# A 128-step state space convolution and a rewritten order of the joint round in a decoder kernel

## The reference, cut to what matters

```
x = layernorm(x_text);  x = x * (1 + gate * scale_in) + gate * shift_in
K = 2 * einsum('dn,dnl->dl', dC, powers).real            # one kernel of L = 256 steps for each channel
y = irfft(rfft(x, n=2L) * rfft(K, n=2L))[:, :L]          # a causal convolution over the 256 steps
y = y + x * D_skip
y = y * (1 + gate * scale_out) + gate * shift_out;  xt = x_text + y
h = gelu(layernorm(xt) @ W1 + b1) @ W2 + b2;  xt = xt + h
```

## Time and profile before

| what | value |
|---|---|
| median of 3 runs | 1935.76 us (1935.62 to 1937.24) |
| the profiled execution | 1936.92 us, span 1935.2 us |
| PE busy / PE weight loads busy | 1686.4 us (87%) / 1308.0 us (68%) |
| DVE / ACT / POOL busy | 1287.0 us (67%) / 864.3 us (45%) / 605.3 us (31%) |
| mean granted TensorE clock | 0.94 of 2.4 GHz |

### The profile page before, as it was taken

One profiled execution on the slowest core, in us unless ns is written; L12 is line 12 of the kernel. 1 busy time (PEld: TensorE's weight loads), 2 busy tenths in 40 slices (PEclk: granted clock), 3 DMA queues, 4 the chain that ended last, 5 costly groups with the idle time before them and its releaser, 6 DMA issues.

```text
span 1935.2 us, 26723 instructions
## 1 busy us (share of the span) xinstructions
PE 1686.4 (87%) x8210; PEld 1308.0 (68%) x8210; DVE 1287.0 (67%) x4141; ACT 864.3 (45%) x1675; POOL 605.3 (31%) x984
## 2 busy tenths in 40 slices
PE   5899999992299999982779999999999999999775
PEld 3677777771166677761658778778778778777654
DVE  3567777762148777334478888889888889876642
ACT  1444444440031111114556766667766667754321
POOL 1111111213300000005534445545444544433211
PEclk9899999995699999995789999999999999999987
DMA  9000000006644343425000000000000000000000
GB/s 272 3 1 1 1 1 1 1 1 234 249 137 137 110 119 99 134 77 197 12 6 1 12 12 6 12 6 12 12 12 6 12 6 7 6 6 1 6 6 11
DMA packets 81573, 94.11 MB, mean 49 GB/s; under 512 B 19142, under 2 KB 69527, under 8 KB 81179
## 3 DMA queue, kind: packets, MB, share of 16 engines
q1 hardware_dynamic: 72747, 78.91, 12.7%
q0 software_dynamic: 3072, 8.39, 1.2%
q10 hardware_dynamic: 5616, 5.11, 0.8%
HBM read 71.94 MB, written 20.45 MB: 48 GB/s over the span
## 4 chain that ended last, share of the span: by engine, by line
PE 35%; DVE 13%; ACT 2%; issue 2%; POOL 2%; POOLq 0%; ACTq 0%
PE E_pY L2313 6%; PE E_pK L2204 5%; PE E_pU L2303 4%; PE E_pK L2163 3%; PE E_pY L2151 3%; PE E_pS L2266 3%; PE E_pY L2284 3%; PE E_pU L2275 2%; DVE E_wk L1738 2%; DVE E_ex L1670 2%; DVE E_m L1731 1%; PE E_pY L2163 1%; PE E_pT L2145 1%; DVE E_num L1677 1%; PE E_pY L2214 1%
## 5 line engine op out<-in xcount | busy, mean ns | idle before, releaser
L1222 ACT ACTIVATE F_uT<-F_puT 128x1024 f32<-128x1024 f32 x39 | 39.9, 1024 | 294.3 <-PE F_puT L1282 294.3
L1492 POOL TENSOR_SCALAR E_var<-E_mv 128x2 f32<-128x2 f32 x80 | 34.2, 427 | 355.9 <-DVE E_mv L1607 355.7
L1273 PE MATMUL F_pu<-C_W,F_hT 128*128 x312 | 143.9, 605 | 0.3 <-issue 0.3
L1291 PE MATMUL F_py<-C_W,F_uT 128*128 x624 | 141.2, 379 | 1.2 <-ACT F_uT L1222 1.2
L1291 PEld LDWEIGHTS F_py<-C_W,F_uT 128*128 128x128 f32 x624 | 115.6, 190 | 16.0 <-issue 1.9
L2214 PE MATMUL E_pY<-E_Wcv,E_hid 128*128 128x256 f32 x512 | 118.7, 386 | 3.3 <-issue 3.3
L2303 PE MATMUL E_pU<-E_xT,E_W 128*128 128x256 f32 x512 | 117.7, 385 | 2.3 <-ACT E_xT L2052 2.3
L2313 PE MATMUL E_pY<-E_W,E_hid 128*128 128x256 f32 x512 | 118.1, 379 | 0.0
L2204 PE MATMUL E_pK<-E_cmix,E_Wck 128*128 128x256 f32 x512 | 115.8, 379 | 1.3 <-ACT E_hid L1993 1.3
L2214 PEld LDWEIGHTS E_pY<-E_Wcv,E_hid 128*128 128x128 f32 x512 | 96.0, 192 | 27.8 <-issue 15.6
L2303 PEld LDWEIGHTS E_pU<-E_xT,E_W 128*128 128x128 f32 x512 | 98.7, 193 | 16.7 <-ACT E_xT L2052 2.9
(11 more groups left out here) (402 smaller groups left out, 4353.9 us busy)
## 6 DMA issues: line engine op xcount, KB each, us to landing
F_b<-in_L_ffn_b SPq DMA_DIRECT2D x39, 512.0 KB, 4.4
C_W<-in_L_ffn_W SPq DMA_DIRECT2D x16, 1024.0 KB, 14.0
sorted_x<-zero SPq DMA_DIRECT2D x1, 4992.0 KB, 19.5
F_xs<-sorted_x SPq DMA_DIRECT2D x39, 128.0 KB, 2.4
F_b<-in_L_ffn_b SPq DMA_DIRECT2D x39, 128.0 KB, 3.1
sorted_y<-F_y ACTq DMA_DIRECT2D x39, 128.0 KB, 2.3
out<-E_tB SPq DMA_DIRECT2D x16, 256.0 KB, 2.1
X<-in_x SPq DMA_DIRECT2D x3, 1024.0 KB, 10.7
```

The source lines that it names most:

```text
L1273: last = nc.tensor.matmul(p_u[:, f, :], hT[:, i % 2, kb, :], W1[:, bass.ds(e, 1), kb, f * 512:(f + 1) * 512], start=kb == 0, stop=kb == KD ...
L1291: last = nc.tensor.matmul(p_y[:, 0:D], uT[:, f, :], W2[:, bass.ds(e, 1), f, :], start=f == 0, stop=f == FB - 1)
```

## The change

**Convolution in two blocks.** The 256 steps become two blocks of 128. Each block is transformed with a real cosine and sine matrix of 128 steps and 128 complex frequencies whose product is circular with a factor i: the real part of a product is what stays in the block, the imaginary part what spills into the next. So `forward` and `inverse` have four matmuls each in place of eight. VectorE forms two products of 1024 elements and two more of 512 (the second half of the kernel on the first block; into tC, which is u, and tD, which is x1). GpSimd has four operations of 512 in place of two. tA gets a tile of its own. `spectrum_product` has four matmuls for eight, and `keep_spectrum` three instructions for one. The loads of the Fourier matrices are a quarter as large.

**Orders.** VectorE's new order in a full round: add_network, film of the second half of the sequence before, difference, norm_out, new_maximum, scores, add_channel_mix, spectrum, take 0, take 1, scale_out, numerator, output, denominator, invert, gated, finish, stats_E, take 2, residual, take 3, average, stats_1, add_mix, film of the first half, keys. TensorE: values before scores; half of channel_out's and network's second halves come earlier; turn_average after half of network's second half; film's two halves later, the second one last in the round. ScalarE: h_1 after the first rectify pair, exps_E behind context instead of ahead of the first square, film's second half last.

**Start and experts.** At the start of the joint stage gather(1) and first(0) come ahead of half of the memsets, and the waits for `init` are split. In the expert blocks bias, turn and gelu are split into two halves of 512 columns with semaphores of their own; `first` runs half by half.

```diff
-            def film(j):
-                dve.wait_ge(e["n1"], j + 1)
-                for t in range(2):
-                    dve.wait_ge(e[f"fp{t}"], j + 1)
+            def film(j, t):
+                if t == 0:
+                    dve.wait_ge(e["n1"], j + 1)
+                dve.wait_ge(e[f"fp{t}"], j + 1)
...
             def spectrum(i):
                 dve.wait_ge(e["Up"], i + 1)
...
-                for part, dst in ((0, tA), (1, tB[:])):
-                    kf = fourier["spec"][:, 2 * part:2 * part + 2, :].rearrange("p b d -> p (b d)")
-                    last = v.tensor_tensor(dst.rearrange("p (a b) d -> p a (b d)", a=2),
...
+                past(dve, d["xx1"], min(i + 2, B - 1))
+                past(dve, d["n2"], min(i + 2, B - 1))
+                for part, dst in ((0, tA[:]), (1, tB[:])):
+                    v.tensor_tensor(dst, p_U[:], fourier["spec"][:, part:part + 1, :].to_broadcast([P, 4, D]), ALU.mult)
+                for part, dst in ((2, tC), (3, tD)):
+                    last = v.tensor_tensor(dst, p_U[:, 0:2], fourier["spec"][:, part:part + 1, :].to_broadcast([P, 2, D]),
+                                           ALU.mult)
                 last.then_inc(e["tAB"], 1)
...
             def spectrum(i):
                 pool.wait_ge(e["tAB"], i + 1)
-                g.tensor_tensor(tA[:, 0:2], tA[:, 0:2], tB[:, 2:4], ALU.subtract).then_inc(e["Y"], 1)
-                g.tensor_tensor(tA[:, 2:4], tA[:, 2:4], tB[:, 0:2], ALU.add).then_inc(e["Y"], 1)
+                chained(g.tensor_tensor(tB[:, 2:4], tB[:, 2:4], tD, ALU.add))
+                chained(g.tensor_tensor(tA[:, 2:4], tA[:, 2:4], tC, ALU.add))
+                settled()
+                g.tensor_tensor(tA[:, 0:4:2], tA[:, 0:4:2], tB[:, 1:4:2], ALU.subtract).then_inc(e["Y"], 1)
+                g.tensor_tensor(tA[:, 1:4:2], tA[:, 1:4:2], tB[:, 0:4:2], ALU.add).then_inc(e["Y"], 1)
...
             def n_E(j):
...
-                past(act, e["Up"], j - 1)
+                if j >= 1:
+                    act.wait_ge(e["Y"], 2 * j)
...
             def forward(i):
...
-                for q in range(4):
-                    for a in range(2):
-                        last = te.matmul(p_U[:, q, :], fourier["fwd"][:, a, q * P:(q + 1) * P], u[:, a, :],
-                                         start=a == 0, stop=a == 1)
+                for a in range(2):
+                    for part in range(2):
+                        last = te.matmul(p_U[:, 2 * a + part, :], fourier["fwd"][:, part * P:(part + 1) * P], u[:, a, :],
+                                         start=True, stop=True)
...
             def inverse(n, i):
...
-                    for q in range(4):
-                        last = te.matmul(p_Y[:, a, :], inv[:, q, a * P:(a + 1) * P], tA[:, q, :],
-                                         start=q == 0, stop=q == 3)
+                    for part in range(2):
+                        last = te.matmul(p_Y[:, a, :], inv[:, part, :], tA[:, 2 * a + part, :],
+                                         start=part == 0, stop=part == 1)
```

170 lines of the change are left out of this document (89 added, 81 removed).

## The result

The changed kernel takes 1917.25 us (median of four runs, 1915.37 to 1922.16), the kernel before beside it 1936.42 (1935.62 to 1937.24). The ratio is 0.9905, 95% interval 0.9886 to 0.9924: faster by 19 us. The forecast was 1883 with a range of 1869 to 1906. The direction was right and the size was not: 55.6 us were added up in the parts, about a third of it came.

What follows compares the result with a forecast made beforehand. PE was taken as the bound, busy 627.28 of 636.78 us in rounds 4 to 15; savings of 32 + 2.3 + 12 + 4.8 + 4.5 = 55.6 from 1936.9 gave 1881.3, and with reserve 1883 us, range 1869 to 1906.

Steps and rivals of the forecast that it cites:

- PE is the bound, and forward and inverse save 1.73 each: Full rounds: PE's order is nearly full; four matmuls for eight, twice a round, save 3.46 us of PE work.
- L1701 (now L1711) falls into a gap of GpSimd's: VectorE operation in finish: meets only the last 0.4 us of a POOL operation, plus 0.4; bounds 0 and 1.2.
- the walk: Full round followed from forward's end through VectorE's new order: average ends at 38.8, turn_average can start at 38.9.
- D: Rival: POOL's four operations and take 0 and take 1 shut each other out of SBUF; beat 61, 1947 us; chance 0.04.
- forecast's sign of 3.1: Profile sign that the forecast is wrong: take 0 or take 1 longer than 3.1 us.
- The beat of 55.0: Full rounds: forward's starts 55.0 us apart instead of 57.89, saving 2.9 a round, 32 in eleven.
- Behind turn_average PE has 52.97 - 37.16 = 15.8 us up to forward's next end.: Full round: PE's pure work a round, less its work up to turn_average, gives the time left behind it.
- 3.1 for the split: Expert blocks: splitting bias, turn and gelu wins 3.1 of the 5.0 us that PE waits for them.
- term of 2.9 for rounds 1 and 2: Start: ACT no longer has exps_E ahead of channel_out's squares, and h_1 is behind the rectify; saves 2.9 us.
- Tail and edges: 12: Rounds 15 to the end: shorter inverse saves 5.2 in rounds 17 and 18, 2 in round 16; 12 us with edges.
- C: Rival: VectorE's pieces from inverse to average take all PE gives up; beat 57.9, only edges count, 1915 us; chance 0.06.
- B: Rival: VectorE late at average by 1.5 us more; beat 56.5, 1899 us; chance 0.2.

Runs made afterwards that it cites:

- no_adds: The changed kernel without GpSimd's two additions of tC and tD, so the spill into the second block is missing from the output; 1915.33 us, ratio 0.9885.
- cover_turn: The changed kernel with turn_E alone moved behind the rest of network on TensorE; 1914.44 us, ratio 0.9872.
- cover_film: cover_both with VectorE's difference moved ahead of film's second half; 1902.67 us, ratio 0.982.
- steady: cover_film, ramp_takes and exps_17 joined, plus n_1, exps_E and n_E moved on ScalarE and six eighths of network's second half ahead of turn_average; 1882.84 us.
- ramp_takes: The changed kernel with take 2 and take 3 of round 2 alone straight behind take 1; 1915.7 us, ratio 0.9888.
- exps_17: The changed kernel with exps_E of round 17 alone in its old place, ahead of the wait for scale_out's norm; 1912.75 us, ratio 0.9874.
- cover_both: The changed kernel with turn_E behind the rest of network and the next round's keys_D ahead of film's second half; 1909.31 us, ratio 0.9845.
- old_orders: The changed kernel with the loops over n of VectorE, ScalarE and TensorE as before the change; 1936.95 us, ratio 1.0005.
- tail_own_max: tail_own with the eight MAX8 of take 2 ahead of scale_out in the full rounds; 1879.08 us, ratio 0.9697.
- steady_tail: steady with rounds 17 and 18 written for themselves, the last sequence's four combining operations on VectorE; 1883.33 us, ratio 0.9708.
- tail_own: steady_tail with the last forward ahead of network's last quarter, norm_out last in VectorE's round 18 order and inverse ahead of turn_6; 1878.41 us, ratio 0.9697.
- steady_tail_max: steady_tail with the eight MAX8 of take 2 ahead of scale_out in the full rounds; 1879.55 us, ratio 0.9688.

## Why the prediction was right or wrong

**PE is the bound, and forward and inverse save 1.73 each.** Right. Each has 8 records of 1.89 us in all, and forward has 1.73 from its start to the next.

**What VectorE and GpSimd get.** Right. The two new products take 0.60 from start to start, VectorE 542.06 / 11 = 49.3 a round (49.4 forecast). GpSimd's result is there 8.9 behind forward's end (8.9). no_adds shows that this chain costs the full rounds nothing.

**L1701 (now L1711) falls into a gap of GpSimd's.** 1.05 us against the 1.1 forecast. Average ends at 39.1 for 38.8; a wait of 0.16 for out_product, which the walk had taken away, is part of that. How much such an operation is drawn out goes by where it begins: L1687 began 1.10 us before the end of GpSimd's operation (1497.22 against 1496.72 + 1.60) and took 0.95 more than the 0.69 of such an operation alone, L1711 began 0.50 before the end of the next (1499.49 against 1498.39 + 1.60) and took 0.36 more, and GpSimd's operation behind that took 1.72 in place of 1.27. The Trainium skill (SBUF — State Buffer, "SBUF: two separate sides") says that whichever of the two starts first has the shared pair of ports for its whole instruction. The trace agrees: each was held up by nearly what the other had left, and the worst case of 1.2 more was not met because L1711 began late in the other's. Take 0 and take 1 run beside GpSimd's four operations. Each of their instructions has its old length (eight MAX8 1.21 and 1.22, a MATCH_REPLACE8 0.22), and D did not come. Take 0 as a whole is 3.15 long, just over the forecast's sign of 3.1, because take 1 starts only 0.25 behind its last replacement where the products started 0.15 behind it before.

**The beat of 55.0.** Wrong, 56.25. The step that failed: "Behind turn_average PE has 52.97 - 37.16 = 15.8 us up to forward's next end." It counted only PE's work there, and the trace shows 17.09. The walk followed VectorE to average with its waits and then stopped; it never asked what turn_E and film's second half wait for once network no longer stands in front of them. The rows of before that would have told it are those of network's two quarters between turn_average, film and turn_E, shown above. cover_turn took 0.77 of the 1.25 back, and with cover_film it is 1.14 (55.11). Cost in eleven rounds: 14 us of the 34 between the forecast of 1883 and the median.

**Waits ahead of turn_average.** turn_1 waits 0.7 and hidden 0.6 for ScalarE, neither in the forecast. They cost nothing in the changed kernel, for PE stood before turn_average anyway; steady, which removes them along with the rest, shows what they are worth when VectorE is no longer alone in setting the place.

**"PE still waits, some 2 us a round, most of it at turn_average."** Wrong in both halves. It is 56.25 - 52.97 = 3.3, and turn_average has 0.28 of it by its bracket (0.4 by starts); the others are turn_1 0.7, hidden 0.6, turn_E 0.78, film 0.6, channel_out 0.2.

**The experts.** spectrum_product saves its 1.73. The 3.1 for the split failed as time, though the waits fell by what was forecast (bias 3.8 to 1.3 us, gelu 1.2 to 0.5, 3.2 together). The forecast took a wait that goes for time that is won. `first` got waits of 0.2 to 0.35 of its own (1.3 in five, 0.3 in one before), and the three middle blocks did not become shorter; 0.4 in the first block and 0.7 in the last are what came, 2.8 with spectrum_product in place of 4.8.

**The start.** The 1.6 for first(0) came: from the last expert block to the first transposes it is 17.83 us for 19.66, and these come 5.4 earlier. The term of 2.9 for rounds 1 and 2 failed. out_product of round 2 still comes 5.9 us earlier (991.11 for 997.00), so ScalarE's squares and the start's lead are real up to there; but VectorE's order, which puts take 2 and take 3 behind finish and residual, holds average of that round until 1004.4. So none of the 9.3 forecast up to forward of round 3 is left (+0.4). The forecast read round 2 from ScalarE's and PE's side only. ramp_takes shows it.

**The tail.** Here the sum has a slip of its own: "Tail and edges: 12" is 5.2 + 2 + 2.5 for the tail, and only with the 2.3 of round 3 does it make 12; the sum adds these 2.3 once more. So the parts were worth 53.3 and not 55.6, and the tail 9.7. That term failed, by 14 in the profiled execution. Round 15 won 0.8 of its 2.5 (53.46 to 52.64), round 16 nothing of its 2 (53.76 and 53.73), and rounds 17 and 18 to the end lost 5.2 where they were to win 5.2. The step "so half of them save 3.3 each, less 0.9 and 0.5" is not what failed in round 17: forward to project is 3.2 shorter there (20.33 to 17.11; 2.4 forecast). In round 18 inverse is 2.8 shorter, but the part ahead of it is 1.6 longer and not 0.5 (12.54 for 10.94).

What failed is that nothing behind project was walked for the rounds without a new sequence. Against the kernel before, round 17 lost 1.8 in project, at the lower clock in this execution (3.75 for 1.97 us), 3.4 for exps_E ahead of turned_3 (shown by exps_17), 2.7 in hidden, which runs at the lower clock behind that wait (gone in exps_17), and 1.7 because turn_average stands behind 24 records of network where it stood behind 16; with the 3.2 won ahead of project that gives the 6.4 by which the round is longer. The forecast named exps_E's move as a gain for the squares in rounds 1 and 2 and did not follow what it was moved ahead of.

**Rivals.** The time fell near C (1915) and the beat near B (56.5), and neither mechanism was it: VectorE was late by what the walk said (39.16 for 38.9), and the full rounds gave 18 us, which C had at nothing.

## What to carry to other kernels

When a piece of filler work is moved from behind a short producer to in front of it, list what stood in its shade: each consumer of the next copy, on each engine, now waits for its own latency, and a sum of pure work behind the last known wait hides that. An order written for the full rounds should be walked again for the first round that has a new member and for the first that lacks one, because there the waits lie elsewhere. Moving one piece out of a wait shifts the next engine's queue: after each move look at what is queued behind the new wait (difference behind film here, 0.6 us a round). And a wait that goes is not yet time won: in the expert blocks 3.2 us of waits went and 1.1 us came of it.

## What the runs showed of the hardware

Two executions with the same tail code differ in it by 3.3 us: from forward of round 17 to that of round 18 the changed kernel took 52.88 us and ramp_takes 49.55. The windows of the same 22 us in both, from 2.2 us ahead of forward of round 17 (columns as in the earlier trace rows; the clock is the third number from the end):

```profile
1801.80:1824.60 22.80, 13.84 (x32) 9.77 (x33) 15.33 (x69) 1.83 (x4) 7.91 (x14) 0.57 0.00 1
```

```profile
1798.50:1821.00 22.50, 13.30 (x40) 8.21 (x40) 18.11 (x80) 2.58 (x5) 9.21 (x14) 0.79 0.01 2
```

The granted clock is 0.57 in the one and 0.79 in the other, and the second gets eight records further. In the first, project takes 3.75 us, in the second 1.96; hidden starts 29.19 and 25.85 behind forward, so the 3.3 all lie ahead of it. exps_17, cover_both and steady have the 3.75 too, cover_turn and cover_film the 1.97, so it does not go with the edits. In the tail a few us of a median can therefore be the clock's, and positions inside a trace, from one forward to the next, tell more than times there; in the full rounds all traces give 1.00, save rounds 4 and 5 of old_orders (0.97), and the periods of one trace mostly agree to a few hundredths of a us.

In tail_own_max the granted clock is 1.00 up to 1718; then PE waits the 1.90 us shown above, and the eight and sixteen records behind take 2.64 and 4.70 us where they take 1.99 and 3.62 behind the same wait in steady, 1.7 us more between them. In the window from 1718.9 to 1730 the clock is 0.85. The wait alone does not decide it: the changed kernel, ramp_takes, exps_17, cover_both, cover_film and steady have the same 1.90 at the same place and 1.99 and 3.62 behind it. In four others (cover_turn, no_adds, steady_tail, tail_own) the same 1.7 us are lost earlier, in scores and forward (2.05 and 2.85 us in tail_own for 1.27 and 1.89, granted clock 0.65 from 1719.6 to 1724.5), and the wait for the channel mix is then only 0.2: there the stretch hides in the wait and costs nothing. From scores of round 16 to forward of round 17 it is 55.05 us in steady, steady_tail and tail_own, and 56.7 in steady_tail_max and tail_own_max, where the stretch falls behind the wait. So the same 1.7 us at the lower level is free ahead of a wait for another engine and paid in full behind it. Why it falls as it does is not shown: both executions that paid it have the MAX8 moved, and that is too few to tell.
